# The last 53 targets' counts move into free columns of the table that picks heavy rows

## What is computed

```python
h = maximum(layernorm(x), 0)
src, dst = edges plus one loop per node
norm = deg_inv_sqrt[src] * deg_inv_sqrt[dst]
for W, b in ((W1, b1), (W2, b2), (W3, b3)):
    h = segment_sum((h @ W)[src] * norm[:, None], dst) + b      # gelu between layers
x = x + h
```

## Time and profile before

| | us |
|---|---|
| median of 3 runs | 2100.68 |
| lowest and highest run | 2097.72, 2101.71 |
| span of the profiled execution | 2094.8 |
| median less that span | 5.9 |
| TensorE busy in the span | 1845.9 |
| VectorE busy in the span | 1538.0 |

### The profile page before, as it was taken

How to read it: one execution, slowest core, us unless ns; L and a number is a source line. 1 busy time by engine, 2 the same in 40 slices (tenths; PEclk the granted TensorE clock), 3 DMA queues, 4 the chain that set the end, 5 groups by cost and what they waited for, 6 DMA issues and landing times. The chain is left out here.

```text
span 2094.8 us, 34290 instructions
## 1 busy us (share of the span) xinstructions
PE 1845.9 (88%) x8860; PEld 1248.4 (60%) x8860; DVE 1538.0 (73%) x4318; ACT 795.2 (38%) x1973; POOL 1268.3 (61%) x1461
## 2 busy tenths in 40 slices
PE   4577887777399999999999979989979999999999
PEld 2344454444155555555555536666647788788777
DVE  7877777776399999999999968988976344335333
ACT  0122222222156656655665536656661121113000
POOL 3777777777788888888888839999977000000000
PEclk7677778887699999999999979999999999999999
DMA  5111111111376666666666762212244343243333
GB/s 160 39 57 50 57 57 57 57 57 54 85 203 194 199 195 195 195 195 198 196 197 194 180 197 74 69 65 69 71 139 128 91 121 118 88 126 114 93 111 107
DMA packets 181734, 254.10 MB, mean 121 GB/s; under 512 B 29276, under 2 KB 144793, under 8 KB 181546
## 3 DMA queue, kind: packets, MB, share of 16 engines
q0 software_dynamic: 47888, 126.25, 21.8%
q1 hardware_dynamic: 104728, 102.31, 15.8%
q10 hardware_dynamic: 28930, 23.35, 3.4%
HBM read 202.35 MB, written 49.37 MB: 120 GB/s over the span
## 5 line engine op out<-in xcount | busy, mean ns | idle before, releaser
L976 POOL DMA_INDIRECT brow<-B_rows,rows x440 | 466.3, 1060 | 115.0 <-issue 59.5
L372 POOL DMA_INDIRECT src_list<-ring,ring_row x392 | 398.4, 1016 | 151.3 <-issue 118.6
L1871 PE MATMUL pO<-F,y 128*128 128x512 f32 x1728 | 435.5, 405 | 8.1 <-DVE y L1696 4.9
L1871 PEld LDWEIGHTS pO<-F,y 128*128 128x128 f32 x1728 | 326.0, 189 | 87.1 <-DVE y L1696 5.2
L1014 PE MATMUL pEdge<-A,turned 128*128 x880 | 333.6, 490 | 0.0
L1234 POOL TENSOR_SCALAR src_oh<-iota,src_s 128x128 bf16<-128x128 bf16 x426 | 283.6, 681 | 41.2 <-PE pC L1403 29.2
L1086 DVE TENSOR_TENSOR pre<-pEdge,brow 128x1024 f32<-128x1024 f32 x220 | 268.8, 1222 | 51.5 <-PE pEdge L1014 41.7
L1023 PE MATMUL pNode<-hid_whole,oh 128*128 128x512 f32 x440 | 227.9, 600 | 4.2 <-DVE sums L1104 3.9
L1692 DVE CAST F<-raw 128x512 fp32r<-128x512 uint16 x432 | 172.9, 437 | 64.6 <-PE pO L1871 60.8
L1048 ACT ACTIVATE turned<-pTurn 128x256 fp32r<-128x256 bf16 x220 | 84.4, 384 | 285.3 <-PE pTurn L1002 285.3
L1279 DVE TENSOR_SCALAR dst_oh<-iota_cw,dst_s 128x458 bf16<-128x458 f16 x568 | 182.3, 368 | 0.0
(11 more groups left out here) (290 smaller groups left out, 3053.5 us busy)
## 6 DMA issues: line engine op xcount, KB each, us to landing
raw<-C_rows SPq DMA_DIRECT2D x71, 768.0 KB, 4.4
C_rows<-c_rows ACTq DMA_DIRECT2D x175, 114.5 KB, 1.7
rows<-src_list SPq DMA_DIRECT2D x110, 100.0 KB, 2.9
brow<-B_rows,rows POOLq DMA_INDIRECT x440, 3.9
U_parts<-part_u SPq DMA_DIRECT2D x25, 256.0 KB, 2.1
B_rows<-bst SPq DMA_DIRECT2D x25, 256.0 KB, 2.1
src_list<-ring,ring_row POOLq DMA_INDIRECT x392
sums<-U_parts SPq DMA_DIRECT2D x17, 256.0 KB, 5.8
```

The source lines that it names most:

```text
L372: nc.gpsimd.indirect_dma_start(dr.src_list[:, :, :].rearrange("p t w -> (p t) w"), bass.IndirectOffsetOnAxis(ap=ring_row[:, k % RING, t:t ...
L976: nc.gpsimd.indirect_dma_start(brow[:, t % BR, :], None, dr.B, bass.IndirectOffsetOnAxis(ap=rows_i[:, m % LCS, j, 1:2], axis=0)).then_inc( ...
L1871: last = mm(pO[m % 2][half][:, :], y[:, win, part, half * P:(half + 1) * P], F[:, n % FS, :], start=(win == 0 and part == 0), stop=False)
```

## The change

F_tail is gone. In layer one, VectorE casts the tail's counts into `pick[:, 0:24, 0:53]`, the free low columns of the pick table, after TensorE has made layer one's picked rows (picks_done 3). Layer one's tail is computed as before, with these columns as weights. In layers two and three `picked(k)` gives in the same 25 products the heavy rows on partitions 64 to 127 of pP_g and the tail's sum over windows 0 to 23 on partitions 0 to 52; `tail(k)` adds one product, that of window 24, to it. So the tail's sum is read from pP_g for k > 0, and the turned tail goes to pL in all layers. The waits follow.

```diff
-        F_tail = g.sb("F_tail", [P, LASTW, TAIL], F32R)
...
             def widen_tail():
                 dve.wait_ge(w_in, 16 * (L + 1))
-                v.tensor_copy(F_tail[:, :, :], raw_tail[:, :, :]).then_inc(tail_ready, 1)
+                dve.wait_ge(picks_done, 3)
+                v.tensor_copy(pick[:, 0:LASTW, 0:TAIL], raw_tail[:, :, :]).then_inc(tail_ready, 1)
...
             def sum_tail(k):
-                v.tensor_tensor(z_tail[:, :], pL[0:TAIL, 0:D], z_low[:, :], ALU.add).then_inc(sum_ready, 1)
+                from_ = pL if k == 0 else pP
+                v.tensor_tensor(z_tail[:, :], from_[0:TAIL, 0:D], z_low[:, :], ALU.add).then_inc(sum_ready, 1)
...
             def read_tail(k):
-                nc.scalar.copy(z_low[:, :], pL[0:TAIL, D:2 * D]).then_inc(low_ready, 1)
+                from_ = pL if k == 0 else pP
+                nc.scalar.copy(z_low[:, :], from_[0:TAIL, D:2 * D]).then_inc(low_ready, 1)
...
             def read_turned(k):
-                nc.scalar.copy(zT_tail[:, :, :], pP[:, 0:P].rearrange("p (k n) -> p k n", k=2)[:, :, 0:TAIL]
+                nc.scalar.copy(zT_tail[:, :, :], pL[:, 0:P].rearrange("p (k n) -> p k n", k=2)[:, :, 0:TAIL]
...
             def picked(k):
+                if k == 1:
+                    pe.wait_ge(tail_ready, 1)
                 if k > 0:
-                    pe.wait_ge(tail_copied, k)
+                    pe.wait_ge(yr_ready, k)
+                    pe.wait_ge(sum_ready, k)
...
             def tail(k):
                 if k == 0:
                     pe.wait_ge(tail_ready, 1)
                     pe.wait_ge(id_ready, 1)
-                else:
-                    pe.wait_ge(sum_ready, k)
-                for win in range(NW):
-                    left = F_tail[:, win, :] if win < LASTW else F_last[:, CHUNKS * CHUNK:N]
-                    last = mm(pL[0:TAIL, :], left, y[:, win, :, :].rearrange("p k n -> p (k n)"), start=(win == 0),
-                              stop=(win == LASTW))
-                last.then_inc(tail_done, 1)
+                    for win in range(LASTW):
+                        mm(pL[0:TAIL, :], pick[:, win, 0:TAIL], y[:, win, :, :].rearrange("p k n -> p (k n)"),
+                           start=(win == 0), stop=False)
+                to = pL if k == 0 else pP
+                mm(to[0:TAIL, :], F_last[:, CHUNKS * CHUNK:N], y[:, LASTW, :, :].rearrange("p k n -> p (k n)"),
+                   start=False, stop=True, skip_group_check=(k > 0)).then_inc(tail_done, 1)
...
             def turn_tail(k):
                 pe.wait_ge(sum_ready, k + 1)
-                pe.wait_ge(yr_ready, k + 1)
+                if k > 0:
+                    pe.wait_ge(tail_copied, k)
                 for half in range(2):
-                    last = nc.tensor.transpose(pP[:, half * (P // 2):half * (P // 2) + TAIL],
+                    last = nc.tensor.transpose(pL[:, half * (P // 2):half * (P // 2) + TAIL],
```

## The result

The changed kernel takes 2087.5 us in the median of 18 runs, the kernel before 2101.0 in 18 beside them. The ratio is 0.9932, with a 95% interval of 0.992 to 0.9943: 12 to 17 us less, about 14.3. On the 2100.68 us that the prediction started from this gives 2086.4 us. I had forecast 2090.2 and a range that began at 2087.0. The sign was right, the gain was larger than forecast.

What follows compares the result with a forecast made beforehand. TensorE was taken as the bound from the end of layer one's chunk 1. Removed products -11.06, lost cover +0.56 and cast 0 make -10.5 us, from 2100.68 to 2090.2 us, range 2087.0 to 2094.3.

Steps and rivals of the forecast that it cites:

- TensorE is the bound in layers two and three: From the end of layer one's chunk 1, each product taken out saves its whole pitch, 0.2304 us for a tail product.
- the terms: Layers two and three: 48 tail products removed, -11.06 us; waits at chunk 2, +0.56; layer one's cast, 0.
- The lost cover: Start of chunk 2, layers two and three: tile 0 waits for ScalarE's copies of chunk 0, 0.28 us a layer.
- The bound of all four copies: Upper bound of chunk 2's opening wait, if all four ScalarE copies had to be done: 1.3 us a layer.
- sum_tail behind the four copies: VectorE in chunk 2: sum_tail waits for z_low behind ScalarE's copies; 1.5 us of slack, so cost nothing.
- The cast in layer one: VectorE's tail cast, now 24 pieces of 53, stays at 1.37 us: change 0, bounds -0.6 and +0.7.
- The spacing of about 131 ns: Skill page's spacing of weight load and product pairs: 48 products worth 6.3 us; the forecast went by the trace's 230 ns.
- that the pitches stay "0.228 and 0.233 as before": Picked and tile products of the dense layers keep their pitches in us; no gain or loss counted.
- Rival 2: Buffers behind F_tail move by 5088 bytes, changing pitches of products reading y: 2086 to 2095 us with 2 ns; chance 0.08.
- no fall of the clock: Rival that the clock falls after chunk 2's new wait, twice +1.8 us, giving 2093.9; chance 0.07.
- layer one's cast in its place: Rival that layer one reacts, by the cast's bounds and its clock fall avoided or doubled: 2087.8 to 2092.7 us; chance 0.05.
- rival 3: The 48 removed tail products are worth only their weight loads, 6.0 us less 0.56, giving 2095.2; chance 0.03.

Runs made afterwards that it cites:

- e1: Changed kernel with an unused 5088-byte allocation where F_tail stood, so every buffer has its address of before; 0.9958 of the kernel before.
- e8: Changed kernel with last_tile(k, 0) of layers two and three made before tile 23 of chunk 1; 0.9907 of the kernel before.
- e2: Kernel before with F_tail declared behind all other buffers, nothing else; 0.9991 of the kernel before.
- e4: Kernel before with a hole of 32 bytes ahead of F_last; 0.9979 of the kernel before.
- e7: Changed kernel with holes of 32 bytes ahead of raw and ahead of F_last; executed once, time not compared, dense stage 526.4 us.
- e3: Changed kernel with a hole of 32 bytes ahead of F_last; executed once, time not compared, dense stage 525.8 us.
- e12: Changed kernel with a hole of 64 bytes ahead of F_last; executed once, time not compared, dense stage 518.8 us.
- e9: Changed kernel with four 32-byte holes making F_last and y, pick and y, zT and w unlike within 64 bytes; time not compared, 96 tile products 21.78 us.

## Why the prediction was right and wrong

- **TensorE is the bound in layers two and three, and a product taken out shortens the run by its pitch: right.** With the addresses held (e1) the stage loses 10.4 us, and the steadier stretch from layer two's picked products 10.5; the terms gave 11.06 - 0.56 = 10.5. From layer two's first product to the end, where the prediction asked for 10 to 11 us less, it is also 10.5 in e1 (355.2 to 344.7), but 15.0 in the changed kernel (340.2). The picked products kept their price, 5.71 in e1 as before.
- **The lost cover: right.** 1.13 us from the first copy to tile 0, 2.12 us for eight products where I had put 2.14; 0.28 a layer forecast and 0.29 measured (2.12 + 0.01 against e8's 1.84; 1.88, the row of before, has the longer pitch in it). The bound of all four copies is excluded by the same row.
- **sum_tail behind the four copies: no wait of TensorE**, as forecast.
- **The cast in layer one: 1.36 us, forecast 1.37.** The broken rows cost nothing, with GpSimd adding b3 beside the cast in both kernels. The page "VectorE: DVE Perf Modes" of the Trainium skill, section "What auto-detection actually checks", lets a one-source copy in SBUF keep its two-port rate if the outermost dimensions of both sides are even or equal; the trace agrees with that.
- **The spacing of about 131 ns**, which the page "TensorE: Matmul & The Clock Gate" of the Trainium skill gives in its section "Back-to-back issue gap", would have made the gain 6.3 us before the wait; e1 shows 10.4 after it. It doesn't hold for these products.
- **Wrong: that the pitches stay "0.228 and 0.233 as before".** This is the step that failed. It was in the sum as zero. The tile products' pitch in a dense row fell by 4.4 ns, because F_tail's removal changed the distance from F to y from 160 to 192 past a multiple of 256. From layer two's picked products on that is worth 4.0 us by either pair of kernels; in the whole stage 5.9 by e1 (526.6 - 520.7) and 4.7 by e2, with 1 us of difference between executions. The forecast's 10.5 and the 5.9 are together the stage's 16.3; by time 14.3 were measured, 12 to 17. Rival 2 named this mechanism, but had a chance of 0.08 and a price of 1 to 2 ns, although the rows held 228, 230 and 233 ns for like products, a spread of 5. I should have read this spread as the size that a shift can have: 5 ns on some 1700 products is 8 us, either way (an estimate). Its 2 ns on 1900 products are 3.8 us, 2086.4 to 2094.0, where the rival says 2086 to 2095. A forecast of -10.5 with a range of -19 to -2 would have been honest.
- The other rivals: no fall of the clock (1.00 after the wait), layer one's cast in its place (1.36 us), and a product is not worth only its weight load (10.5 us in e1, where rival 3 had 6.0 less 0.56).

Had F_tail not stood ahead of y, the change would have given 10 us. Had the layout been the other way round, with y at a short distance before and a long one after, part of it would have been lost and the change judged a small one: from e4 (stage 530.4) to e7 (526.4) the same change brings 4.0 us, from e2 (532.3) to e3 (525.8) 6.5.

## What to carry to other kernels

An edit that removes or resizes a buffer moves all buffers behind it, and a product's pitch can move with them: read the pitch of products that the change does not touch in both traces before explaining the time, and keep the addresses with a hole of the same size when an edit is to be measured by itself. Price removed products by their pitch in a stretch without idle time, and ask at once which wait they had covered: here, the wait for the banks' copies came out and took 5% of the gain. Where what lies ahead of a stage varies more than the effect, compare the stage from a fixed instruction to the end, and let it start where one engine is the bound throughout: from layer two's picked products on, executions of one kernel agree to 0.1 us, from `slot` on only to 1. And an average pitch over a short row mixes the row's own with that of what stood ahead: read the last products of a long row.

## What the runs showed of the hardware that I had not expected

The pitch of a pair of weight load (128 columns) and product of 512 fp32r columns, in a dense row, is 0.2267, 0.2291 or 0.2333 us, depending on the distance of the two operands' buffers modulo 256 bytes: 0 shortest, 192 next, the other four tried longest and alike to 0.0002. After a row of another kind it takes some nine products until that pitch is reached (e12 and the changed kernel, above). The rule is shown for 128 weight columns alone. Layer one's tail, 24 products with 53 weight columns that now lie in the table's rows, a multiple of 256 from y, takes 5.64 us (0.235 each), more than before with F_tail (5.76 for 25, 0.230), whose rows of 212 bytes put each product at another distance; in e9, with pick and y unlike, it takes 5.58. That costs 0.1 us once, and wasn't followed further.
